# Causal mask of the plain attention scores: from TensorE's accumulation to VectorE's row-max operation

## The chip, the cores and the metric

The kernel runs on one core of a Trainium2 chip, in one launch. The metric is device time in microseconds (us). The kernel before was run three times: 2249.01, 2249.69 and 2251.82 us; its time is the median, 2249.69 us. One further execution was profiled.

## The reference, cut to what matters

Two layers of a gated cross-attention model with routed experts, on 16 sequences (batches) of 256 tokens, width 256. Only layer 0's attention changes:

```python
qh = (q @ Wq.T) ...; kh = (k @ Wk.T) ...; vh = (v @ Wv.T + bv) ...      # 16 heads of 16
scores = einsum('bhsd,bhtd->bhst', qh, kh) * scale
mask = triu(ones((Sq, Sq)), k=0).at[0, 0].set(False)
scores = where(mask, -inf, scores)
probs = softmax(scores, axis=-1)
out = einsum('bhst,bhtd->bhsd', probs, vh)
```

A token sees only the tokens before it (the first one sees itself). Layer 0's experts, layer 1's attention (with a length mask in place of the causal one) and layer 1's experts follow; the change leaves them alone.

## The kernel before, in words

The program is a row of phases: a short setup, then for each layer an attention phase, a routing phase and an expert phase. A phase begins when the one before it has ended, so a microsecond taken from layer 0's attention is one taken from the whole.

`attention_phase` (the function printed below) runs the five engines as parallel programs, tied by semaphores. Each is a software pipeline over the 16 batches (`pipeline`, with `step(i)`); in one step an engine works on several batches at once: `i.at(0)` is the batch whose output is formed, `i.at(1)` the one whose row maxima are found, `i.at(2)` the one whose queries and keys are projected, `i.at(3)` and `i.at(4)` those that are turned, normalized and loaded.

Scores are computed twice for each head. The **plain scores** (queries on partitions) serve only for the maximum of each row. The **turned scores** (keys on partitions) are computed again with the row maximum as extra rows of the stacked operands, so that ScalarE can take the exponential at once (L629) and TensorE can use the result as the operand of the product with the values (L788). In this text s(h) stands for the plain scores of head h of the next batch, t(h) for the turned scores of head h of the present batch.

Plain scores of a head fill three blocks of 128 columns of one PSUM bank: queries 0-127 by keys 0-127, queries 128-255 by keys 0-127, and queries 128-255 by keys 128-255. Before the change TensorE writes them with five matmuls of 128 columns each (L742 to L746): for the first and the third block a matmul of the identity with `mask_st` writes the mask (-1e30 above and on the diagonal), and the score matmul is added to it in PSUM. The turned scores are formed in the same way (L760 to L764). There are two banks for plain scores: s(h) waits until the maxima of head h-2 are taken (`maxed`, L738). Likewise t(h) waits for the exponential of head h-2 (L756).

The order of one step, written out by hand, is what the prediction follows:

- TensorE: query projection of `i.at(2)` (L670), turning of the max parts (L696), key projection (L670), then for h = 0 to 15: s(h), t(h); after head 4 the output projection (L711), after 6 the value projection (L679), after 8 and 9 the turnings (L660), and after heads 5, 9, 13 and 15 the products with the values of four heads (`mix_group`, L788).
- VectorE: the key copy (L470), then for each head two row maxima (L547 on 128 columns, L548 on 256), and between heads one other operation: reciprocals and divisions (L492, L498), the update of x (L507), the value copy (L517), the low parts of the turned rows (L524), the layer norm (L434, L439, L446). At the end of the step the 16 heads' maxima are cut into three bf16 parts (L558 to L565).
- ScalarE: the query copy (L605), the copy of the turned max parts (L610), and the three DMAs that lay them into `q_stack` (L614); then the 16 exponentials, with cuts and copies between them.
- t(0) waits for those three DMAs (L755).

Of the kernel before, what the change touches and what calls it, by code (L numbers as in the profile page):

```python
# [140 lines left out]
def attention_phase(nc, keep, layer, x_in, ctx_in, lens, weights, biases, scratch):  # L141
# [31 lines left out]
    with ExitStack() as ctx:  # L173
        def sb(name, shape, dt=F32):
            return ctx.enter_context(nc.sbuf_tensor(tag + name, shape, dt))
# [42 lines left out]
        if causal:  # L218
            mask_st = sb("mask_st", [P, 2, P], BF16)
            mask_ts = sb("mask_ts", [P, 2, P], BF16)  # L220
            bv_rows = sb("bv_rows", [P, TC, D])
            bo_rows = sb("bo_rows", [P, D])
        else:
            lens_i = sb("lens_i", [P, B], I32)
            lens_f = sb("lens_f", [P, B])
            iota_t = sb("iota_t", [P, S])
            neg_col = sb("neg_col", [P, 1])
            valid = sb("valid", [P, S])
            mask_row = pair("mask_row", [P, S], BF16)
# [43 lines left out]
        stacked = [sems(f"stacked_half{n}_") for n in range(2)]  # L273
        scores_done = sem("scores_done")
        maxed = sem("maxed")
        max_hi = sem("max_hi")
# [81 lines left out]
        def _(pool):  # L358
# [6 lines left out]
            if causal:  # L365
# [4 lines left out]
                nc.gpsimd.affine_select(out=mask_st[:], in_=mask_st[:], compare_op=ALU.is_gt, fill=CAUSAL_FILL,  # L370
                                        base=0, pattern=[[0, 2], [-1, P]], channel_multiplier=1).then_inc(consts_step, 1)
                nc.gpsimd.affine_select(out=mask_ts[:], in_=mask_ts[:], compare_op=ALU.is_gt, fill=CAUSAL_FILL,
                                        base=0, pattern=[[0, 2], [1, P]], channel_multiplier=-1).then_inc(consts_step, 1)
                pool.wait_ge(consts_step, 5)
                nc.gpsimd.memset(mask_st[0:1, 0, 0:1], 0.0).then_inc(consts_step, 1)
                nc.gpsimd.memset(mask_ts[0:1, 0, 0:1], 0.0).then_inc(consts_step, 1)
                pool.wait_ge(consts_step, 7)
            else:
# [37 lines left out]
        def _(dve):  # L416
# [67 lines left out]
            def step(i):  # L484
# [55 lines left out]
                for h in range(H):  # L540
                    if h == 11 and i.has(4):
                        dve.wait_ge(stats_done, i.at(4) + 1)
                    if i.has(1):
                        dve.wait_ge(scores_done, i.at(1) * H + h + 1)
                        bank = scores[h % 2]
                        if causal:
                            nc.vector.reduce_max(row_max[:, 0, h:h + 1], bank[:, 0:P], AX_X)  # L547
                            nc.vector.reduce_max(row_max[:, 1, h:h + 1], bank[:, P:3 * P], AX_X).then_inc(maxed, 1)  # L548
                        else:
                            nc.vector.reduce_max(row_max[:, :, h], bank[:].rearrange("p (c t) -> p c t", c=TC), AX_X).then_inc(maxed, 1)  # L550
                    if h in between:
                        between[h]()
# [83 lines left out]
        def _(pe):  # L636
# [97 lines left out]
            def score_head(i, h):  # L734
# [6 lines left out]
                if causal:  # L741
                    nc.tensor.matmul(bank[:, 0:P], keep.ident16[:], mask_st[:, 0, :], start=True, stop=False)  # L742
                    nc.tensor.matmul(bank[:, 0:P], q[rows, h, 0:P], k[rows, h, 0:P], start=False, stop=True)
                    nc.tensor.matmul(bank[:, P:2 * P], q[rows, h, P:S], k[rows, h, 0:P], start=True, stop=True)
                    nc.tensor.matmul(bank[:, 2 * P:3 * P], keep.ident16[:], mask_st[:, 1, :], start=True, stop=False)
                    last = nc.tensor.matmul(bank[:, 2 * P:3 * P], q[rows, h, P:S], k[rows, h, P:S], start=False, stop=True)  # L746
                else:
# [1091 lines left out]
```

## Time and profile before

| | us |
|---|---|
| median of three runs | 2249.69 |
| profiled execution, its own time | 2242.63 |
| its span from first to last instruction | 2240.9 |
| outside the span | 1.7 |

The mean granted TensorE clock over the span is 0.874 of full speed (2.4 GHz). Layer 0's attention takes about the first 560 us of the span. The profile names engines PE (TensorE matmul), PEld (its weight loads, which overlap), DVE (VectorE), ACT (ScalarE), POOL (GpSimd) and SP (SyncE). Matmuls are pipelined: the durations of their rows overlap, and the distance between starts is what one costs in a dense stretch. VectorE's rows overlap too, by a smaller amount.

### The profile page before, as it was taken

How to read it: one execution, taken by the hardware profiler on the slowest of the kernel's cores; microseconds unless marked ns; L12 is line 12 of the kernel's file. 1: busy time of each engine (PE TensorE's matmuls, PEld its weight loads, DVE VectorE, ACT ScalarE, POOL GpSimd, SP SyncE). 2: the span in 40 equal slices, each digit the busy share in tenths (PEclk: the TensorE clock that was granted, in tenths of full speed). 3: DMA queues.
4: the chain of work that ended last, by engine and by line, in shares of the span. 5: the costliest groups of instructions: out<-in, count | busy, mean ns of one | idle time of the engine just before them, and what ended most of it. 6: DMA issues, size and time to landing. Idle time of an engine off the chain costs nothing. (4 is left out here: it accounts for less than half of the span.)

```text
span 2240.9 us, 44334 instructions
## 1 busy us (share of the span) xinstructions
PE 1637.9 (73%) x14427; PEld 1343.8 (60%) x14428; DVE 1236.0 (55%) x3261; ACT 665.6 (30%) x1299; POOL 724.0 (32%) x620
## 2 busy tenths in 40 slices
PE   3787778887575477735877877787463888896897
PEld 3676667665464355533555555554342888886897
DVE  3565556554466133344656656654465566667664
ACT  2233333333464011111433333343232222221221
POOL 4121112210476455541111111110386533334332
PEclk9989998998898799976888988988676999998999
DMA  3323333321222366644323323320622233332322
GB/s 105 106 88 89 90 104 88 87 78 31 102 94 99 83 116 107 107 91 111 92 84 91 96 78 87 89 74 16 217 78 76 61 66 75 75 75 66 75 35 40
DMA packets 166676, 191.78 MB, mean 86 GB/s; under 512 B 15442, under 2 KB 146868, under 8 KB 166324
## 3 DMA queue, kind: packets, MB, share of 16 engines
q1 hardware_dynamic: 135092, 149.69, 22.9%
q0 software_dynamic: 28416, 40.03, 9.9%
q10 hardware_dynamic: 3072, 0.79, 0.2%
q8 instruction: 59, 0.97, 0.2%
q14 instruction: 37, 0.30, 0.0%
HBM read 113.73 MB, written 75.67 MB: 85 GB/s over the span
## 5 line engine op out<-in xcount | busy, mean ns | idle before, releaser
L629 ACT ACTIVATE a_probs<-a_scores_t 128x384 f32<-128x384 f32 (+1 forms) x512 | 269.7, 545 | 524.7 <-PE a_scores_t L764 262.4
L1714 ACT ACTIVATE e_hidden<-e_h,t_up_bias 128x256 f32<-128x256 f32 x348 | 145.9, 470 | 564.7 <-PE e_h L1748 552.5
L550 DVE TENSOR_REDUCE a_row_max<-a_scores 128x2 f32<-128x512 f32 x256 | 170.3, 679 | 170.5 <-PE a_scores L749 169.0
L407 POOL TENSOR_TENSOR a_rest<-a_qk,a_parts 128x1024 f32<-128x1024 f32 x32 | 68.0, 2125 | 461.6 <-ACT a_parts L582 461.6
L1639 POOL DMA_INDIRECT out_rows<-e_y,e_token x68 | 112.5, 1654 | 309.9 <-DVE e_y L1697 289.9
L1763 PE MATMUL e_y_bank<-e_down_hi,e_hidden_hi 128*128 128x256 f32 x544 | 165.1, 304 | 64.2 <-DVE e_hidden_lo L1670 63.2
L767 PE MATMUL a_scores_t<-a_q_stack,a_k_stack 101*128 101x256 bf16 x512 | 115.7, 315 | 69.0 <-DMA a_q_stack<-a_max_t 67.2
L547 DVE TENSOR_REDUCE a_row_max<-a_scores 128x1 f32<-128x128 f32 x256 | 71.5, 279 | 168.7 <-PE a_scores L746 167.4
L1763 PE MATMUL e_y_bank<-e_down_hi,e_hidden_lo 128*128 128x256 f32 x544 | 159.6, 293 | 0.0
L1763 PE MATMUL e_y_bank<-e_down_lo,e_hidden_hi 128*128 128x256 f32 x544 | 159.4, 293 | 0.0
L1748 PE MATMUL e_h<-e_xs_hi,e_up_hi 128*128 128x256 f32 x544 | 155.9, 287 | 3.1 <-DVE e_xs_lo L1660 1.9
L1670 DVE TENSOR_TENSOR e_hidden_lo<-e_hidden,e_hidden_hi 128x512 fp32r<-128x512 f32 x136 | 153.9, 1132 | 4.7
L1748 PE MATMUL e_h<-e_xs_hi,e_up_lo 128*128 128x256 f32 x544 | 155.3, 285 | 1.4 <-issue 1.4
L1748 PE MATMUL e_h<-e_xs_lo,e_up_hi 128*128 128x256 f32 x544 | 155.3, 285 | 0.4 <-issue 0.4
L1639 POOL DMA_INDIRECT x_mid_dram<-e_y,e_token x76 | 118.0, 1553 | 105.6 <-DVE e_y L1697 72.6
L1763 PEld LDWEIGHTS e_y_bank<-e_down_hi,e_hidden_hi 128*128 128x128 f32 x544 | 110.4, 203 | 69.1 <-DVE e_hidden_lo L1670 68.9
L749 PE MATMUL a_scores<-a_k_stack,a_q_stack 98*128 98x256 bf16 x512 | 115.9, 315 | 33.3 <-DMA a_k_stack<-a_mask_row 16.1
L788 PE MATMUL a_pv<-a_probs,a_v_pad 128*32 128x256 f32 (+1 forms) x2048 | 123.5, 358 | 21.4 <-ACT a_probs L629 21.4
L1151 POOL DMA_INDIRECT routed_rows_dram<-r_rows,r_slot x128 | 126.4, 987 | 38.0 <-issue 35.4
L1692 DVE TENSOR_TENSOR e_y_biased<-e_y_bank,t_down_bias 128x512 f32<-128x512 f32 x72 | 49.8, 692 | 151.4 <-PE e_y_bank L1763 135.0
L492 DVE RECIPROCAL a_den_recip<-a_pv 128x128 f32<-128x128 f32 x128 | 120.4, 944 | 18.1 <-PE a_pv L788 18.1
L1726 PE MATMUL e_turned<-ident,e_xs_rows 128*128 128x128 f32 x296 | 47.9, 285 | 105.6 <-DMA e_xs_rows<-routed_rows_dram 105.4
(257 smaller groups left out, 4539.9 us busy)
## 6 DMA issues: line engine op xcount, KB each, us to landing
parts_dram<-a_parts SPq DMA_DIRECT2D x32, 768.0 KB, 4.1
e_xs_rows<-routed_rows_dram SPq DMA_DIRECT2D x76, 258.0 KB, 2.7
a_q_stack<-parts_dram SPq DMA_DIRECT2D x64, 192.0 KB
a_k_stack<-parts_dram SPq DMA_DIRECT2D x64, 192.0 KB
a_ctx_rows<-in_ctx SPq DMA_DIRECT2D x32, 256.0 KB, 9.1
a_q_stack<-parts_dram SPq DMA_DIRECT2D x64, 128.0 KB
a_k_stack<-parts_dram SPq DMA_DIRECT2D x64, 128.0 KB
t_up<-in_L_ffn_W SPq DMA_DIRECT2D x8, 1024.0 KB, 5.2
```

What stands on the lines that cost most here:

```text
L492: nc.vector.reciprocal(den_recip[:, m, cols], pv[m][:, S + part * P:S + part * P + P]).then_inc(recip_done, 1)
L550: nc.vector.reduce_max(row_max[:, :, h], bank[:].rearrange("p (c t) -> p c t", c=TC), AX_X).then_inc(maxed, 1)
L629: nc.scalar.activation(probs[h % NP][:, 0:width], scores_t[h % 2][:, 0:width], ACT.Exp).then_inc(probs_ready, 1)
L749: last = nc.tensor.matmul(bank[:, c * S:(c + 1) * S], q[rows, h, c * P:(c + 1) * P], k[rows, h, :], start=True, stop=True)
L767: last = nc.tensor.matmul(bank[:, c * S:(c + 1) * S], k[rows, h, c * P:(c + 1) * P], q[rows, h, :], start=True, stop=True)
L788: last = nc.tensor.matmul(bank[n * VW:(n + 1) * VW, what * S + first:what * S + S], rows, probs[h % NP][:, col:col + S - first], start=(ha ...
L1151: pool.indirect_dma_start(out=xs, out_offset=bass.IndirectOffsetOnAxis(ap=slot[p][:, k, c:c + 1], axis=0), in_=rows[p][:, k, c, :], in_off ...
L1639: pool.indirect_dma_start(out=x_acc, out_offset=bass.IndirectOffsetOnAxis(ap=token[p][:, c:c + 1], axis=0), in_=y[p][:, c, :], in_offset=N ...
L1670: nc.vector.tensor_tensor(lo, src, hi.bitcast(F32), ALU.subtract).then_inc(hidden_cut, 1)
L1714: nc.scalar.activation(hidden[:, fc, :], h_bank[g][:, at:at + TS], act_func, bias=routed.up_bias[:, bass.ds(e * FC + fc, 1)]).then_inc(hid ...
L1748: last = nc.tensor.matmul(h_bank[g][:, at:at + TS], w[:, kc, fc * P:(fc + 1) * P], x[:, kc, :], start=(kc == 0 and term == 0), stop=(kc == ...
L1763: last = nc.tensor.matmul(y_bank[:, c * D:(c + 1) * D], x[:, fc, c * P:(c + 1) * P], w[:, fc, :], start=(fc == 0 and term == 0), stop=(fc ...
```

## The change

The plain scores lose their two mask matmuls, and the two blocks of queries 128-255, which share the stationary operand, become one matmul of 256 columns: two matmuls for a head in place of five. VectorE's two `reduce_max` become two `tensor_tensor_reduce`, which read the scores and the mask, write the masked scores back into the PSUM bank, and give the row maximum as accumulated output. `mask_st` becomes float32 with a third block: triangle, zeros, triangle. The wait for the scores now stands at a separate semaphore instruction (`head_taken`, which nothing waits for) in front of the pair. Turned scores, layer 1 and all else are unchanged.

```diff
-            mask_st = sb("mask_st", [P, 2, P], BF16)
+            mask_st = sb("mask_st", [P, 3, P])
...
+        head_taken = sem("head_taken")
...
                 nc.gpsimd.affine_select(out=mask_st[:], in_=mask_st[:], compare_op=ALU.is_gt, fill=CAUSAL_FILL,
-                                        base=0, pattern=[[0, 2], [-1, P]], channel_multiplier=1).then_inc(consts_step, 1)
+                                        base=0, pattern=[[0, 3], [-1, P]], channel_multiplier=1).then_inc(consts_step, 1)
...
                 nc.gpsimd.memset(mask_st[0:1, 0, 0:1], 0.0).then_inc(consts_step, 1)
+                nc.gpsimd.memset(mask_st[:, 1, :], 0.0).then_inc(consts_step, 1)
                 nc.gpsimd.memset(mask_ts[0:1, 0, 0:1], 0.0).then_inc(consts_step, 1)
-                pool.wait_ge(consts_step, 7)
+                pool.wait_ge(consts_step, 8)
...
                     if i.has(1):
-                        dve.wait_ge(scores_done, i.at(1) * H + h + 1)
                         bank = scores[h % 2]
                         if causal:
-                            nc.vector.reduce_max(row_max[:, 0, h:h + 1], bank[:, 0:P], AX_X)
-                            nc.vector.reduce_max(row_max[:, 1, h:h + 1], bank[:, P:3 * P], AX_X).then_inc(maxed, 1)
+                            dve.wait_ge(scores_done, i.at(1) * H + h + 1)
+                            dve.sem_inc(head_taken, 1)
+                            nc.vector.tensor_tensor_reduce(bank[:, 0:P], bank[:, 0:P], mask_st[:, 0, :], 1.0, CAUSAL_FILL,
+                                                           ALU.add, ALU.max, row_max[:, 0, h:h + 1])
+                            nc.vector.tensor_tensor_reduce(bank[:, P:3 * P], bank[:, P:3 * P],
+                                                           mask_st[:, 1:3, :].rearrange("p a b -> p (a b)"), 1.0, CAUSAL_FILL,
+                                                           ALU.add, ALU.max, row_max[:, 1, h:h + 1]).then_inc(maxed, 1)
...
                 if causal:
-                    nc.tensor.matmul(bank[:, 0:P], keep.ident16[:], mask_st[:, 0, :], start=True, stop=False)
-                    nc.tensor.matmul(bank[:, 0:P], q[rows, h, 0:P], k[rows, h, 0:P], start=False, stop=True)
-                    nc.tensor.matmul(bank[:, P:2 * P], q[rows, h, P:S], k[rows, h, 0:P], start=True, stop=True)
-                    nc.tensor.matmul(bank[:, 2 * P:3 * P], keep.ident16[:], mask_st[:, 1, :], start=True, stop=False)
-                    last = nc.tensor.matmul(bank[:, 2 * P:3 * P], q[rows, h, P:S], k[rows, h, P:S], start=False, stop=True)
+                    nc.tensor.matmul(bank[:, 0:P], q[rows, h, 0:P], k[rows, h, 0:P], start=True, stop=True)
+                    last = nc.tensor.matmul(bank[:, P:3 * P], q[rows, h, P:S], k[rows, h, :], start=True, stop=True)
```

## Rows read from the trace of the kernel before

**Rows 1.** The page, part 1: busy time of each engine over the span.
```profile
PE 1637.9 (73%) x14427; PEld 1343.8 (60%) x14428; DVE 1236.0 (55%) x3261; ACT 665.6 (30%) x1299; POOL 724.0 (32%) x620
```
**Rows 2.** Stretches: us, then PE, PEld, DVE, ACT, POOL busy, PEclk, DMA.
```profile
240.75:247.00 6.25, 6.25 (x53) 6.05 (x54) 3.44 (x10) 3.29 (x6) 2.13 (x1) 0.66 0.05 18
...
240.75:272.49 31.74, 25.41 (x343) 21.69 (x343) 18.53 (x53) 11.30 (x22) 6.43 (x5) 0.93 0.33 93
```
**Rows 3.** Waits from 60 to 540 us: us in total, times, longest.
```profile
DVE a_row_max L547 <- PE a_scores L746: 155.8, 108, 4.7
...
PE a_scores_t L760 <- DMA a_q_stack<-a_max_t: 59.0, 15, 4.7
```
**Rows 4.** Timeline of TensorE, one step: start us, us, what, [idle before <-releaser].
```profile
207.98 0.29 PE L760 MATMUL a_scores_t<-a_mask_ts,ident 128*128 128x128 bf16 x1 [4.69 <-DMA a_q_stack<-a_max_t]
...
211.68 0.31 PE L742 MATMUL a_scores<-a_mask_st,ident 128*128 128x128 bf16 x1
...
212.75 2.74 PE L711 MATMUL a_stage<-a_wo_t,a_heads_t 128*128 128x256 f32 x8
...
223.71 0.22 PE L742 MATMUL a_scores<-a_mask_st,ident 128*128 128x128 bf16 x1
...
224.29 0.22 PE L742 MATMUL a_scores<-a_mask_st,ident 128*128 128x128 bf16 x1
...
226.28 0.23 PE L742 MATMUL a_scores<-a_mask_st,ident 128*128 128x128 bf16 x1 [0.66 <-DVE a_row_max L548]
...
233.37 0.29 PE L696 MATMUL a_stage<-ident,a_max_parts 128*48 128x128 bf16 x2
...
240.75 0.29 PE L760 MATMUL a_scores_t<-a_mask_ts,ident 128*128 128x128 bf16 x1 [4.57 <-DMA a_q_stack<-a_max_t]
```
**Rows 5.** Timeline of VectorE in the same step, the same columns.
```profile
210.81 0.41 DVE L548 TENSOR_REDUCE a_row_max<-a_scores 128x1 f32<-128x256 f32 x1
...
224.20 0.29 DVE L547 TENSOR_REDUCE a_row_max<-a_scores 128x1 f32<-128x128 f32 x1 [1.32 <-PE a_scores L746]
224.40 0.41 DVE L548 TENSOR_REDUCE a_row_max<-a_scores 128x1 f32<-128x256 f32 x1
224.74 0.74 DVE L434 BATCH_NORM_STATS2 a_stats<-x_rows 128x6 f32 x2
225.60 0.29 DVE L547 TENSOR_REDUCE a_row_max<-a_scores 128x1 f32<-128x128 f32 x1
...
228.89 0.29 DVE L547 TENSOR_REDUCE a_row_max<-a_scores 128x1 f32<-128x128 f32 x1 [0.24 <-PE a_scores L746]
...
232.74 0.19 DVE L565 TENSOR_TENSOR a_max_parts<-a_max_rest,a_max_parts 128x32 bf16<-128x32 f32 x1
```
**Rows 6.** Timeline of ScalarE at the end of that step.
```profile
233.47 0.60 ACT L605 ACTIVATE a_qk<-a_stage 128x512 f32<-128x512 f32 x1 [3.22 <-PE a_stage L670]
233.97 0.36 ACT L610 ACTIVATE a_max_t<-a_stage 48x256 bf16<-48x256 bf16 x1
```
**Rows 7.** Layer 1's score matmul, line 749: ns min/median/max, first and last start.
```profile
L749 PE MATMUL a_scores<-a_k_stack,a_q_stack x512: 270/275/437, 1039.1 to 1541.1; 98*128 98x256 bf16 x171
```
**Rows 8.** Timeline of ScalarE in layer 1's routing: squares with an accumulated sum.
```profile
1595.46 0.38 ACT L1375 ACTIVATE r_proj_sq<-r_gated 128x256 f32<-128x256 f32 x1 [3.98 <-PE r_gated L1430]
1595.74 0.19 ACT L1375 ACTIVATION_READ_ACCUMULATOR r_proj_sq<-r_gated 128x1 f32 x1
1595.83 0.38 ACT L1375 ACTIVATE r_proj_sq<-r_gated 128x256 f32<-128x256 f32 x1
```
**Rows 9.** Groups by line and shape, 60 to 540 us: busy us, mean ns.
```profile
L517 DVE TENSOR_TENSOR a_v_pad<-a_stage,a_bv_rows 128x512 f32<-128x512 f32 x16 | 10.9, 680 | 0.0
```
**Rows 10.** The page, part 5: the expert phase's subtraction of two SBUF operands.
```profile
L1670 DVE TENSOR_TENSOR e_hidden_lo<-e_hidden,e_hidden_hi 128x512 fp32r<-128x512 f32 x136 | 153.9, 1132 | 4.7
```
**Rows 11.** Timeline of GpSimd in the setup: its last constant.
```profile
13.67 0.10 POOL L385 MEMSET a_var_eps<- 128x2 f32 x1
```
**Rows 12.** Timeline of VectorE in the setup: its last fills.
```profile
16.12 0.12 DVE L422 MEMSET a_ones_pad<- 128x16 f32 x3
```

More of the change, by code:

```diff
@@ L543, in step @@
                     if i.has(1):
-                        dve.wait_ge(scores_done, i.at(1) * H + h + 1)
                         bank = scores[h % 2]
                         if causal:
-                            nc.vector.reduce_max(row_max[:, 0, h:h + 1], bank[:, 0:P], AX_X)
-                            nc.vector.reduce_max(row_max[:, 1, h:h + 1], bank[:, P:3 * P], AX_X).then_inc(maxed, 1)
+                            dve.wait_ge(scores_done, i.at(1) * H + h + 1)
[5 more added lines that the diff above has]
+                                                           ALU.add, ALU.max, row_max[:, 1, h:h + 1]).then_inc(maxed, 1)
                         else:
+                            dve.wait_ge(scores_done, i.at(1) * H + h + 1)
                             nc.vector.reduce_max(row_max[:, :, h], bank[:].rearrange("p (c t) -> p c t", c=TC), AX_X).then_inc(maxed, 1)
```

## Prediction

> **What bounds the kernel now.** I read the page first: TensorE is busy 73% of the span, VectorE 55%, and no engine is full [rows 1]. Such an average says nothing of one phase, so I went to layer 0's attention alone. It repeats with a period, from the start of t(0) in one step to that of the next: 207.98 to 240.75, 240.75 to 272.49 [rows 2, 4]. In the second of these TensorE's rows fill 25.4 of 31.7 us, VectorE's 18.5. The waits over this phase say where the two hand over: VectorE waits 155.8 us for plain scores, in 108 of its heads, and TensorE waits 59.0 us in 15 pieces for the DMAs of the max parts [rows 3]. So a period has two parts.
>
> The **fixed part** is a chain: last row maximum, max parts (end of L565, 232.93), turning L696 (233.37), copy L610 (233.97), DMAs, t(0) at 240.75 [rows 4 to 6]. From L610 on it is 6.78 us of latency in which TensorE mostly idles. The change touches none of it.
>
> The **part of heads** runs from t(0) to L610, 26.0 us. There the timeline of TensorE shows matmuls back to back, except at one place: s(13) at 226.28 waits 0.66 us for VectorE [rows 4]. In front of it VectorE has a full row: head 10 at 224.20, the layer-norm statistics, head 11 at 225.60 [rows 5]. It is TensorE's part with VectorE close behind, and that closeness decides this change.
>
> **What TensorE saves.** From s(10) at 223.71 to s(11) at 224.29 lie ten matmuls in 0.58 us: 0.058 each [rows 4]. A 256-column matmul of layer 1 lasts 275 ns against 220 for 128 columns [rows 4, 7], that is one such step more, so the merged matmul costs what its two halves did, and a head saves the two mask matmuls: 0.115 us at 2.4 GHz, 0.213 at 1.2. s(0) lies in front of the DMA wait and saves nothing. At most 15 heads by 0.115, or 1.7 us a period, and 26 us in all over 15 periods.
>
> **What VectorE pays**, called x for a head. Before, a pair holds it 0.54 us (224.20 to 224.74), and its result is there after 0.62 (224.20 to the end of L548) [rows 5]. Streaming a second operand costs nothing: 512 columns with a PSUM and an SBUF input take 680 ns, 267 more than L548's 0.41 for 256, 1.04 ns a column, as the reductions do [rows 5, 9]. The accumulated output is the new cost. No row shows it on VectorE. On ScalarE it is an instruction of its own that puts the next start off by 0.09 us (1595.74 to 1595.83) [rows 8]. VectorE's fixed share of an instruction is 0.07 (0.20 from L547 to L548, less 128 columns at 1.04 ns), so I take 0.07 for each read and 0.01 for the pair's second operands: x = 0.15. Bounds: 0, if the read hides in the pipeline; 0.30, if each read must wait for the end of its operation (0.09 later, by L547's 0.29 against 0.20). Writing back to PSUM instead of SBUF is shown by no row; between nothing and the same 0.30 bound I take nothing.
>
> The Trainium skill, "VectorE: DVE Perf Modes", section "Two Vector instructions with no wait between them", says that an op which also writes out its accumulator is two instructions. It gives no price. Were it wrong, x would be 0.01, and the sum some 20 us down.
>
> **The separate wait.** Scores reach VectorE 0.04 us after the last matmul (it starts at 223.71 + 4 x 0.058 = 223.94, lasts 0.22, and VectorE starts at 224.20) [rows 4, 5]. Behind a wait that its sequencer holds, as head 11 behind the wait for the statistics, the start comes 0.12 after the release (225.48 to 225.60) [rows 5]. So y = 0.08 for each head whose scores VectorE awaits, and nothing where it is behind; bounds 0 and 0.15. Queued behind it stand VectorE's other operations, which are then late by as much.
>
> **The sum for one period**, in three stretches.
> *First, t(0) to the output projection (207.98 to 212.75)*, at the low clock: the granted clock of the like stretch is 0.66 [rows 2]. Masks of four heads go. The clock's rise stays about where it is, so columns count at the high clock: 4 x 0.115 = 0.46. Against it, s(4) would come at 211.68 - 3 x 0.213 = 211.04, but the maxima of head 2 end at 211.22 now [rows 4, 5], and then at 211.22 - 0.21 + y + 2x = 211.39 and a little: a wait of 0.4, worth 0.2 of high-clock work. Net -0.26.
> *Second, s(5) to s(10).* Dense on TensorE, with projections and value products that give VectorE room: 5 x 0.115 = -0.58.
> *Third, s(10) to L610.* Times from s(10) on. Scores of head 10 after 0.06 + 0.275, seen at 0.46 (before 0.49). Pair 0.69, statistics 0.92, pair result 0.76, release 0.05: s(13) at 2.88 instead of 2.57. VectorE goes on without idling: head 11 starts at 2.07, head 14 follows 3.29 - 0.24 of idling + 3x later, at 5.57 instead of 5.18 [rows 5]; the max parts end 4.04 + 2x + 0.04 after that, at 9.95 instead of 9.22. L696 and L610 follow at 0.03, 0.29 and 0.05: L610 at 10.32 instead of 10.26. The gap of 0.4 between L565's end and L696 is thus used up; the other input of L610's turn, the query projection and L605, is early by then. Net +0.08: a stretch in which three more heads' masks save nothing.
> Together -0.76. Twelve of the 15 periods have this form: -9.1. In the next two, whose steps load nothing further and leave out the layer norm, -1.4; in the last, where TensorE already waits for the maxima, -0.5. The first 16 heads, which have no turned scores beside them, are paced by the two banks; shorter scores and longer maxima cancel within 0.04 a pair: +0.3. **Sum -10.7 us.**
>
> Costed at nothing: the wider float32 mask in the setup, under 1 us more on GpSimd, which finishes at 13.8 while VectorE's fills of the same wait end at 16.2 [rows 11, 12]; without that cover it would cost its full length once. The extra `head_taken` increments have no waiter. No DMA changes.
>
> The profiled execution would go from 2242.63 to 2231.9 (span 2230.2). It stands 7.1 us under the median of the three runs, a spread I can't attribute, so against the median: 2249.69 - 10.7 = 2239.0. A difference under about 0.2% (4.5 us) can't be told from none here.
>
> **The rivals.**
> *VectorE becomes the bound (slower).* Third-stretch time grows by 6x and the first by about x: 7 us for each us of x and period, so the gain is gone at x = 0.15 + 0.76/7 = 0.26, and any more is a loss. At x = 0.30 a period is 0.29 longer, 4 us in all: 2254. For: x rests on another engine's row. 
> *TensorE stays the bound (x near 0).* Then the first stretch gives 0.46, the third 0.33 and the second 0.58: 1.4 by 15, about 20 us: 2229 (in the third, s(13) comes at 2.59, and the masks of three more heads count). Chance 0.08.
> *The clock gives it back.* TensorE has fewer columns and two new short waits in a phase whose clock falls in every period (0.66 after the wait, 0.93 over all [rows 2]). One us more at 1.2 GHz costs 0.5 us of work a period, 7.5 us in all: 2246, within 0.2%. For: periods already differ by 1 us (32.8 and 31.7) with the same work. Chance 0.20.
>
> **How the numbers follow.** Forecast 0.47; with x near 0, faster is 0.55; within 0.2% is the clock's 0.20; slower 0.25. Time 2239.0. The range takes in x near 0 with a little clock luck at its low end (2226) and x = 0.30 with the clock's 7.5 us at its high end (2262); the half-rate case is left out. The forecast's own range is 2231 to 2244.
>
> **What the profile would show.** Right: two plain score matmuls a head, of 128 and 256 columns, at the old pace; VectorE's pair at 0.65 to 0.72 us, with two short reads; a longer wait of TensorE at s(13) and a new one at s(4); L610 to t(0) still 6.3 to 6.8; VectorE's 155.8 us of waiting for scores down by a third or more; nothing changed after the phase. Wrong: a pair over 0.8 us, no read rows, periods shorter by over 1.2, a granted clock under 0.92 in the periods, or a longer DMA wait.

## The result, and the profile after

The changed kernel took 2256.26 us (median of 20 runs, 2248.97 to 2262.76), the kernel before 2249.52 us (20 runs beside them). The ratio is 1.0029, 95% interval [1.0020, 1.0039]: slower by 4.5 to 8.8 us, where -10.7 us was forecast. On another chip (experiment 9 below) it was 1.0034 [1.0020, 1.0049]. The profiled execution of the changed kernel has a span of 2253.9 us and a mean granted clock of 0.857, where before had 2240.9 and 0.874.

In the changed kernel the plain matmuls are L749 (128 columns) and L750 (256), VectorE's pair L550 and L552, the turned scores L764 to L768, the output projection L718, the turning of the max parts L703 and its copy L617. The page's first part, against [rows 1]:

```profile
PE 1625.8 (72%) x13659; PEld 1310.1 (58%) x13660; DVE 1256.0 (56%) x3773; ACT 664.4 (29%) x1299; POOL 724.5 (32%) x621
```

TensorE lost 768 matmuls and only 12 us of busy time; VectorE gained 512 instructions and 20 us. Its groups by line and shape, 60 to 540 us (busy us, mean ns of one, then idle time before them):

```profile
L552 DVE CUSTOM_DVE_ANT_0 a_scores<-a_scores,a_mask_st 128x256 f32<-128x256 f32 x247 | 115.1, 466 | 0.0
L550 DVE CUSTOM_DVE_ANT_0 a_scores<-a_scores,a_mask_st 128x128 f32<-128x128 f32 x247 | 73.6, 298 | 146.8 <-PE a_scores L750 141.5 <-DVE a_stats L436 4.0
L552 DVE DVE_READ_ACCUMULATOR2_ANT a_row_max<- 128x1 f32 x247 | 35.2, 142 | 0.0
```

and the same of the kernel before:

```profile
L548 DVE TENSOR_REDUCE a_row_max<-a_scores 128x1 f32<-128x256 f32 x253 | 104.6, 413 | 0.0
L547 DVE TENSOR_REDUCE a_row_max<-a_scores 128x1 f32<-128x128 f32 x252 | 70.3, 279 | 157.1 <-PE a_scores L746 155.8
```

Each fused operation has its read as a row of its own. What such a read costs is seen in VectorE's timeline at head 10, against the pair of [rows 5]:

```profile
225.32 0.30 DVE L550 CUSTOM_DVE_ANT_0 a_scores<-a_scores,a_mask_st 128x128 f32<-128x128 f32 x1 [0.73 <-PE a_scores L750]
225.53 0.14 DVE L550 DVE_READ_ACCUMULATOR2_ANT a_row_max<- 128x1 f32 x1
225.53 0.47 DVE L552 CUSTOM_DVE_ANT_0 a_scores<-a_scores,a_mask_st 128x256 f32<-128x256 f32 x1
225.91 0.14 DVE L552 DVE_READ_ACCUMULATOR2_ANT a_row_max<- 128x1 f32 x1
225.91 0.75 DVE L436 BATCH_NORM_STATS2 a_stats<-x_rows 128x6 f32 x2
```

The read starts in the same instant as the operation behind it, so it puts nothing off. The pair holds VectorE 0.59 us (225.32 to 225.91; 0.54 before). Its result is there after 0.73 us (to the end of the second read; 0.61 before).

**Where the time went** is in the stages of one period. Stretches of the kernel before, from t(0), s(4), s(5) and s(10), the last one up to the copy of the max parts (us; PE, PEld, DVE, ACT, POOL busy; granted clock; DMA share, GB/s). s(5) is at 215.32:

```profile
207.98:211.68 3.70, 3.70 (x35) 3.70 (x36) 2.42 (x8) 2.31 (x4) 0.38 (x1) 0.50 0.07 25
211.68:215.32 3.64, 3.64 (x20) 3.15 (x19) 1.02 (x4) 0.98 (x2) 1.75 (x1) 0.63 0.00 0
215.32:223.71 8.39, 8.39 (x135) 7.03 (x134) 4.78 (x13) 3.85 (x7) 2.14 (x1) 1.00 0.32 94
223.71:233.97 10.26, 8.71 (x140) 6.84 (x137) 8.23 (x26) 3.71 (x9) 2.16 (x3) 1.00 0.44 117
```

The same of the changed kernel (its last one runs on to the key projection, 0.25 us past the copy at 235.06):

```profile
208.96:212.42 3.46, 3.27 (x26) 2.82 (x26) 2.23 (x10) 2.34 (x5) 0.34 (x1) 0.50 0.07 25
212.42:216.77 4.35, 4.35 (x16) 3.38 (x16) 1.50 (x9) 0.84 (x2) 1.79 (x1) 0.50 0.00 0
216.77:224.80 8.03, 8.03 (x121) 6.53 (x120) 5.19 (x23) 3.85 (x7) 2.14 (x1) 0.97 0.32 91
224.80:235.31 10.51, 8.19 (x123) 6.11 (x120) 8.68 (x38) 4.04 (x9) 2.16 (x3) 1.00 0.47 120
```

and TensorE's timeline there, against [rows 4]:

```profile
208.96 0.29 PE L764 MATMUL a_scores_t<-a_mask_ts,ident 128*128 128x128 bf16 x1 [4.54 <-DMA a_q_stack<-a_max_t]
...
212.42 0.29 PE L749 MATMUL a_scores<-a_k_stack,a_q_stack 96*128 96x128 bf16 x1 [0.19 <-DVE a_row_max L552]
...
213.25 3.73 PE L718 MATMUL a_stage<-a_wo_t,a_heads_t 128*128 128x256 f32 x8
...
224.80 0.22 PE L749 MATMUL a_scores<-a_k_stack,a_q_stack 96*128 96x128 bf16 x1
...
226.12 0.23 PE L749 MATMUL a_scores<-a_k_stack,a_q_stack 96*128 96x128 bf16 x1 [0.25 <-DVE a_row_max L552]
...
227.73 0.23 PE L749 MATMUL a_scores<-a_k_stack,a_q_stack 96*128 96x128 bf16 x1 [0.99 <-DVE a_row_max L552]
...
241.74 0.29 PE L764 MATMUL a_scores_t<-a_mask_ts,ident 128*128 128x128 bf16 x1 [4.58 <-DMA a_q_stack<-a_max_t]
```

The output projection starts 4.29 us after t(0), 0.48 earlier than before (4.77): the saving is there. But it now runs wholly at 1.2 GHz (3.73 us against 2.74), and 3.52 us pass from its start to s(5) instead of 2.57. The granted clock is 0.50 in both first stretches and still 0.97 in the third; in the kernel before it had risen within the second (0.63). These rows put the loss down to the clock, and the experiments test it.

The period shown is one in which the clock rises late in both kernels. Over periods 1 to 12, the first after t(0) of batch 0 being period 0, the projection starts 4.41 us after t(0) before and 4.29 after, a saving of only 0.12, and from there to s(5) pass 1.97 and 3.11 us. The rise from 1.2 to 2.4 GHz comes 4.4 us after t(0) in the kernel before (3.1 to 6.4) and 7.2 in the changed one (6.1 to 8.6). That is more than where the fall happens to lie. Where the clock had fallen 1.6 to 2.6 us before t(0), it stayed low for 6.8 us in the kernel before (all three such periods) and in kernel 7 below (all five), and for 10.2 in the changed one (all five). TensorE also pauses in front of s(4) in all twelve periods of the changed kernel, by 0.39 to 0.40 us from one matmul's start to the next beyond their usual distance, and in none of the kernel before.

Between 75 and 550 us TensorE spent 86 us at 1.2 GHz before and 125 after. The expectations below say 85 and 132 for this; those were read from the same clock records in a window set 10 us early.

The waits from 60 to 540 us, against [rows 3]:

```profile
DVE a_scores L550 <- PE a_scores L750: 141.5, 84, 5.7
PE a_scores_t L764 <- DMA a_q_stack<-a_max_t: 55.5, 15, 4.7
...
PE a_scores L749 <- DVE a_row_max L552: 23.4, 49, 1.4
```

The last of them was 10.3 us in 18 pieces before: TensorE now waits for the maxima 49 times. The DMA wait stayed.

The 15 periods together, from copy to copy of the max parts, went from 467.4 to 473.9 us: +6.5, against +6.7 between the medians. The two profiled executions differ by more, 13.0 us of span. Of this 6.9 had come by the end of the attention phase (573.6 and 580.5), and 6.1 lie behind it, where the code is the same (1667.3 and 1673.5 us). In the four kernels of experiments 1 to 4 that same code took between 1666.0 and 1673.3 us, so I take the 6.1 as spread, not as the change's.

### The profile page after: what moved, and what is told of

It is laid out like the page before. It is cut to its first block and busy times, and to the rows that moved or that the text cites. A ratio compares the mean times of both kernels' runs of the same rounds, so it can differ in the third digit from the quotient of the medians.

```text
span 2253.9 us, 43564 instructions
## 1 busy us (share of the span) xinstructions
PE 1625.8 (72%) x13659; PEld 1310.1 (58%) x13660; DVE 1256.0 (56%) x3773; ACT 664.4 (29%) x1299; POOL 724.5 (32%) x621
## 5 line engine op out<-in xcount | busy, mean ns | idle before, releaser
L409 POOL TENSOR_TENSOR a_rest<-a_qk,a_parts 128x1024 f32<-128x1024 f32 x32 | 68.0, 2125 | 457.2 <-ACT a_parts L589 457.2
L550 DVE CUSTOM_DVE_ANT_0 a_scores<-a_scores,a_mask_st 128x128 f32<-128x128 f32 x256 | 76.4, 298 | 160.5 <-PE a_scores L750 155.2
```

## Experiments

Two theories. **Clock:** both halves of the change cost or save about what was forecast, but together they leave TensorE with too little to do after the DMA wait, and the high clock comes later. **VectorE:** its longer, later maxima simply hold TensorE up, and the clock only shows that. The twelve runs stand on three chips, on which the kernel before takes 2249.23 (runs 1 to 4), 2232.24 (5 to 8) and 2231.20 us (9 to 12). So kernels are compared by their ratios to it, or within one chip.

The table gives what each left: ratio with interval, the mean over periods 1 to 12 of the stretches in us ("wait" is copy of the max parts to t(0); "1st" t(0) to s(5); "2nd" s(5) to s(10); "3rd" s(10) to the next copy), the mean time from t(0) to the rise of the clock, the time at 1.2 GHz from 75 to 550 us, and the 15 periods together. Where the wait is filled the table gives wait and first stretch together (12.93 before, 14.02 changed); t(0) is then the first matmul behind the filling, and "rise" tells in how many of the twelve periods the clock was low during the filling. From t(0) to s(5) it was high in all of them. Each row's stretches come from one profiled execution.

| kernel | ratio to before | wait | 1st | 2nd | 3rd | rise | 1.2 GHz | 15 periods |
|---|---|---|---|---|---|---|---|---|
| before | 1 | 6.56 | 6.37 | 8.39 | 10.20 | 4.4 | 86 | 467.4 |
| changed | 1.0029 [1.0020, 1.0039] | 6.63 | 7.39 | 7.90 | 10.25 | 7.2 | 125 | 473.9 |
| 1 VectorE's half | 1.0045 [1.0028, 1.0063] | 6.60 | 6.54 | 8.39 | 10.73 | 4.8 | 90 | 478.3 |
| 2 TensorE's half | 0.9907 [0.9890, 0.9924] | 6.74 | 6.25 | 7.78 | 9.73 | 5.0 | 106 | 450.8 |
| 3 changed, filled | 0.9910 [0.9894, 0.9926] | 12.08 | with wait | 7.78 | 10.25 | none | 21 | 451.6 |
| 4 before, filled | 0.9933 [0.9917, 0.9950] | 12.08 | with wait | 8.39 | 10.20 | once | 14 | 456.4 |
| 5 TensorE's half, filled | 0.9891 [0.9865, 0.9918] | 12.52 | with wait | 7.79 | 9.73 | twice | 28 | 446.6 |
| 6 VectorE's half, filled | 1.0001 [0.9990, 1.0012] | 12.22 | with wait | 8.39 | 10.73 | none | 12 | 467.0 |
| 7 columns, heads 0-4 | 0.9995 [0.9980, 1.0010] | 6.70 | 6.30 | 7.78 | 10.65 | 4.3 | 100 | 465.8 |
| 8 held wait alone | 1.0007 [0.9996, 1.0018] | 6.67 | 6.47 | 8.39 | 10.42 | 4.7 | 85 | 473.6 |
| 9 changed again | 1.0034 [1.0020, 1.0049] | 6.64 | 7.21 | 7.87 | 10.25 | 6.8 | 123 | 471.4 |
| 10 as 7, again | 0.9991 [0.9977, 1.0005] | 6.73 | 6.28 | 7.78 | 10.38 | 4.2 | 101 | 463.7 |
| 11 columns, two places | 0.9983 [0.9968, 0.9999] | 6.72 | 6.29 | 7.78 | 10.36 | 4.0 | 91 | 462.9 |
| 12 as 3, again | 0.9929 [0.9912, 0.9946] | 12.08 | with wait | 7.78 | 10.38 | none | 23 | 451.8 |

**1. VectorE's half alone.** VectorE as in the changed kernel, TensorE with its five matmuls, the two mask operands zeros:

```diff
-                    nc.tensor.matmul(bank[:, 0:P], keep.ident16[:], mask_st[:, 0, :], start=True, stop=False)
+                    nc.tensor.matmul(bank[:, 0:P], keep.ident16[:], zero_st[:], start=True, stop=False)
...
-                    nc.tensor.matmul(bank[:, 2 * P:3 * P], keep.ident16[:], mask_st[:, 1, :], start=True, stop=False)
+                    nc.tensor.matmul(bank[:, 2 * P:3 * P], keep.ident16[:], zero_st[:], start=True, stop=False)
```

> VectorE as in the changed kernel (mask and maximum in one operation, separate wait); TensorE as before, with five matmuls a head, of which the two that wrote the mask now write zeros. Theory C (the clock): what the change lost, it lost because TensorE, with fewer columns and a pause at s(4) after the DMA wait, is granted its high clock later. With the columns back, the time at the low clock between 75 and 550 us returns from 132 us to about 85, the stretch from t(0) to s(5) from 7.35 us to about 6.5 a period, and the whole stands at 0 to 8 us over the kernel before, which is VectorE's own price. Theory V (VectorE's longer pair and its held wait set the pace): the loss of 6.7 us stays and the 10 to 15 us that the dropped masks saved are added: 16 us or more over the kernel before, and low-clock time stays above 120 us.

Measured: 2258.58 us against 2249.23, +10.1 us by the ratio, above the 0 to 8 of theory C and below the 16 of theory V. The clock's rise at 4.8 us and the first stretch (6.54) are near those of before.

**2. TensorE's half alone.** The two matmuls of the changed kernel, VectorE with its two reductions:

```diff
-                    nc.tensor.matmul(bank[:, 0:P], keep.ident16[:], mask_st[:, 0, :], start=True, stop=False)
-                    nc.tensor.matmul(bank[:, 0:P], q[rows, h, 0:P], k[rows, h, 0:P], start=False, stop=True)
...
+                    nc.tensor.matmul(bank[:, 0:P], q[rows, h, 0:P], k[rows, h, 0:P], start=True, stop=True)
+                    last = nc.tensor.matmul(bank[:, P:3 * P], q[rows, h, P:S], k[rows, h, :], start=True, stop=True)
```

> Plain scores are not masked at all (two matmuls a head, reduce_max as before, the wait on the reduction itself), so the row maxima are taken over all keys; the turned scores keep their mask. This has TensorE's saving without VectorE's price. Theory V: nothing is left that costs, the whole saving shows: 15 to 25 us under the kernel before. Theory C: stretches two and three gain (0.6 and 0.3 a period), but the clock's rise is late in part here too, since the columns are missing: low-clock time over 100 us between 75 and 550, and 3 to 13 us under the kernel before.

Measured: 2229.09 us, -20.9 us by the ratio. The time is what theory V expected (15 to 25 under) and not theory C's 3 to 13, although the low clock lasted 106 us, as C had it: TensorE's half alone loses little to the clock. The halves alone give +10.1 and -20.9, together -10.8 (by the 15 periods +10.9 and -16.6, together -5.7), and in one kernel they give +6.5. In the **third stretch** they do add: +0.53 and -0.47, and the changed kernel has +0.05. In the second, -0.61 and 0 against -0.49. In the **first** they do not: +0.17 and -0.12 against +1.02. Neither half alone moves the rise of the clock by over 0.6 us; both together move it by 2.8. Nor does either half alone show the pause in front of s(4): it is under 0.1 us in kernel 2, and 0.07 and 0.17 in two periods of kernel 1.

**3 and 4. The wait filled.** In the changed kernel and in the kernel before, 34 matmuls of 256 columns, whose result is overwritten, stand in front of the wait for the max parts (not for the first batch, where the phase has no such wait behind it):

```diff
+                if h == 0:
+                    if causal and not (isinstance(b, int) and b == 0):
+                        for _ in range(34):
+                            nc.tensor.matmul(bank[:, 0:2 * P], keep.ident16[:], mask_ts[:].rearrange("p a b -> p (a b)"), start=True, stop=True)
+                    pe.wait_ge(max_stacked[p], (i.half(0) + 1) * 48)
```

> The changed kernel with 34 matmuls of 256 columns (identity by a constant, result overwritten) put on TensorE into its wait for the DMAs of the max parts, so that it isn't idle there; work is added, none is left out. Theory C: the clock no longer falls in the periods, low-clock time between 75 and 550 us drops from 132 to under 30 us, the stretch from t(0) to s(5) from 7.35 to about 5 us, and the kernel is 25 to 35 us faster than the changed one, 18 to 28 under the kernel before. Theory V: VectorE sets the first stretch, the filling changes it by under 0.5 us a period, and the kernel stays within 7 us of the changed one.

> The kernel before with the same 34 filling matmuls in the same wait. Theory C: its low-clock time of 85 us goes too, the stretch from t(0) to s(5) falls from 6.4 to about 5.3 us: 12 to 20 us under the kernel before. Against the previous run (the changed kernel, filled) it then stands at plus 5 to 12 us, the change's gain with the clock out of the way, as forecast. Theory V: the filled kernel before is faster than the filled changed kernel.

Measured: 2228.27 and 2233.19 us, by their ratios 20 and 15 us under the kernel before. The timeline of TensorE in kernel 3:

```profile
257.22 3.88 PE L763 MATMUL a_scores_t<-a_mask_ts,ident 128*128 128x256 bf16 x34
261.85 0.23 PE L767 MATMUL a_scores_t<-a_mask_ts,ident 128*128 128x128 bf16 x1 [0.76 <-DMA a_q_stack<-a_max_t]
```

and its stretches from the copy of the max parts (255.30), the filling and the output projection:

```profile
255.30:257.22 1.92, 1.68 (x14) 1.65 (x15) 0.00 (x0) 0.36 (x2) 0.00 (x0) 1.00 0.65 204
257.22:265.38 8.16, 6.51 (x69) 5.28 (x67) 4.85 (x19) 2.58 (x5) 1.05 (x1) 1.00 0.20 62
265.38:267.16 1.78, 1.78 (x11) 1.49 (x9) 1.04 (x7) 0.49 (x1) 1.08 (x1) 1.00 0.00 0
```

The true t(0) starts at 261.85, 6.55 us after the copy, here no later than without the filling (6.78 against 6.63 over the twelve periods). The clock falls in none of the twelve periods, and 1.78 us pass from the output projection's start to s(5) instead of 3.52. Same masks, same VectorE, same DMAs: what differs is the clock, and the changed kernel's loss becomes a gain.

With the clock held the change is worth 4.9 us over kernel 4 (4.8 in the 15 periods), though the two intervals overlap. That is just under the 5 to 12 expected, and half of the 10.7 that the prediction had. The twelve periods show where: the first stretch is 5.17 us in kernel 4 and 5.30 in kernel 3, so it loses 0.13 where it was to gain.

**5 and 6. The halves with the wait filled.** The same filling in kernel 2 and kernel 1.

> Plain scores unmasked (two matmuls a head, reduce_max), and the DMA wait filled with the 34 matmuls; only the mask of the row maxima is left out. Theory C: with the clock held in all of them, savings and prices add up. The filled kernel before is 16 us under the unfilled one; TensorE's saving of 1.1 to 1.5 us a period comes in full on top: 30 to 40 us under the kernel before. Theory V: the unmasked kernel had nothing to lose on VectorE already, and filling adds what it gave the kernel before: about 36 us under. Both give nearly the same here; it is run as the version that could beat the others, and as a corner for the next run.

> VectorE's new operations, TensorE's five matmuls (zeros for the mask), DMA wait filled. Theory C: the price of VectorE's side alone with the clock held is as without filling, 7 to 11 us over the filled kernel before (which is 16 under the kernel before), so 5 to 9 us under the kernel before; and the four filled kernels (both sides old, either new, both new) fit a sum of two terms within 4 us, where the four unfilled ones miss it by 17. Theory V: they miss it by over 10 us here too, since VectorE's price would depend on how early the scores come, whatever the clock.

Measured: 2209.38 and 2232.48 us against 2232.24. Kernel 5 is the fastest of all, but leaves the mask of the maxima out. Both missed. Kernel 5 was to be 30 to 40 us under the kernel before and is 24 by its ratio; kernel 6 was to be 5 to 9 under and is level with it. Nor do the four filled kernels fit a sum of two terms within 4 us. From kernels 4, 5 and 6 the changed one, filled, should take 457.2 us for the 15 periods, and it took 451.6. By the ratios, which here stand on two chips, the miss is 11 us.

The stretches say why. Mean us over the twelve periods, with the wait apart:

| filled kernel | wait | 1st | 2nd | 3rd |
|---|---|---|---|---|
| 4 before | 6.92 | 5.17 | 8.39 | 10.20 |
| 6 VectorE's half | 6.68 | 5.54 | 8.39 | 10.73 |
| 5 TensorE's half | 7.61 | 4.91 | 7.79 | 9.73 |
| 3 changed | 6.78 | 5.30 | 7.78 | 10.25 |

With the clock held all three stretches add, the first one too: +0.37 and -0.26, and the whole has +0.13. VectorE's half costs 0.90 us a period, 0.37 in the first stretch and 0.53 in the third, and 0.91 with the masks gone (kernel 3 against kernel 5). That is 11 us over twelve periods, as in the 15 periods of kernel 6 against kernel 4 (10.6).

What does not add is the wait, and this is the filling's own cost. In kernel 5 the filling began 2.8 to 4.3 us after the copy, and in 11 of the twelve periods t(0) followed its last matmul at once, 0.11 us behind it; t(0) came 0.87 us later than in kernel 2 (7.61 against 6.74). There the filling itself delayed t(0), by most in the two periods in which the clock was low during it (9.45 and 9.70 us). In kernel 4 this happened in three periods, one at the low clock (9.52), in kernels 3 and 6 in two each. One period of kernel 5, where s(0) waits for the key transfer and the filling stands behind s(0):

```profile
257.32 0.23 PE L742 MATMUL a_scores<-a_k_stack,a_q_stack 96*128 96x128 bf16 x1 [0.95 <-DMA a_k_stack<-parts_dram]
257.50 3.88 PE L756 MATMUL a_scores_t<-a_mask_ts,ident 128*128 128x256 bf16 x34
261.21 0.22 PE L760 MATMUL a_scores_t<-a_mask_ts,ident 128*128 128x128 bf16 x1
```

**7. Columns put back after the wait only.** The changed kernel with two matmuls of 128 zero columns in heads 0 to 4 (s(0) lies in front of the wait, so eight of the ten stand behind it):

```diff
+                    fill = h <= 4 and i.has(0)
+                    if fill:
+                        nc.tensor.matmul(bank[:, 0:P], keep.ident16[:], zero_st[:], start=True, stop=False)
+                    nc.tensor.matmul(bank[:, 0:P], q[rows, h, 0:P], k[rows, h, 0:P], start=not fill, stop=True)
+                    if fill:
+                        nc.tensor.matmul(bank[:, 2 * P:3 * P], keep.ident16[:], zero_st[:], start=True, stop=True)
```

> The changed kernel with two 128-column matmuls of zeros put back into the plain scores of heads 0 to 4 of each step alone, those that follow the DMA wait. Theory C, columns decide when the clock rises: low-clock time between 75 and 550 us falls from 132 to under 105 us, the stretch from t(0) to s(5) from 7.4 to about 6.6 us, and the kernel is 5 to 12 us faster than the changed one (0 to 6 us under the kernel before), though it does more work. Rival P, the pause at s(4) decides and not the columns: low-clock time stays over 120 us, and the kernel is as slow as the changed one or up to 4 us slower.

**8. The held wait alone.** The kernel before with the separate semaphore instruction in front of its reductions:

```diff
                         if causal:
+                            dve.sem_inc(head_taken, 1)
                             nc.vector.reduce_max(row_max[:, 0, h:h + 1], bank[:, 0:P], AX_X)
```

> The kernel before with only the separate semaphore instruction in front of reduce_max (five matmuls, masks and reductions as before). It prices the wait that VectorE's sequencer holds: from the changed kernel's rows the start comes 0.20 us after the last matmul's end in place of 0.04. If the wait is the larger part of VectorE's price (9 us with the masks kept): 5 to 9 us slower than the kernel before, third stretch up by 0.3 us. If the longer operations are the larger part: under 4 us slower, third stretch up by under 0.2.

Measured: kernel 7 2232.45 us, level with before; its rise at 4.3 us and its first stretch (6.30) are back at those of before, with VectorE as slow as in the changed kernel. That rules out that VectorE's longer maxima alone make the loss. It does not separate theory C from rival P, for the added matmuls also take up the time of the pause: in front of s(4) it is gone (under 0.02 us in eleven periods, 0.11 in one).

Kernel 8 took 2234.40 us, +1.6 us by its ratio [-0.9, +4.0], with +0.22 in the third stretch of the 0.53 that VectorE's half costs there. At head 10 its reduction starts 0.15 us after the last matmul's end in all twelve periods, against 0.04 before and 0.19 in the changed kernel. By time and third stretch the held wait is the smaller part of VectorE's 10 us; but the 15 periods of its one profile are 6.2 us longer than those of before, so its share is not settled.

Kernel 7's third stretch surprised: 12.0 to 12.3 us in three of the twelve periods, 10.2 to 10.5 in the others. One of the three:

```profile
187.55:199.84 12.29, 9.78 (x122) 6.77 (x119) 8.67 (x38) 3.78 (x8) 2.16 (x3) 0.86 0.41 104
```

The granted clock is 0.86 there: it fell once more, at 190.91, when TensorE had waited 1.35 us for VectorE at s(13) (190.84). Four kernels on one chip followed.

**9. The changed kernel again.**

> The changed kernel again, on the chip of the three kernels beside it, since the eight runs so far stand on two chips whose kernel before differs by 17 us. Clock theory: ratio to before 1.001 to 1.005; the low clock between 75 and 550 us lasts about 132 us against 85, the first stretch about 7.4 us against 6.4. Rival (the loss came with one chip, and the change is a gain elsewhere): ratio 0.997 or less with the same stretches.

**10. Kernel 7 again.**

> The changed kernel with the two dropped matmuls (128 columns each, zeros) put back in heads 0 to 4 alone, again. Clock theory: some 3 to 8 us under the changed kernel beside it (first stretch 6.3 against 7.4 us, given back in part in the third, where three of twelve periods of the earlier run took 12 us instead of 10.25, each with a low clock between heads 12 and 15). Rival (the columns cost what they take and the clock gives nothing): 0 to 3 us over the changed kernel.

**11. Columns in both sparse places.** Kernel 7 with one line changed:

```diff
-                    fill = h <= 4 and i.has(0)
+                    fill = (h <= 4 or 11 <= h <= 13) and i.has(0)
```

> The same columns put back in heads 0 to 4 and in heads 11 to 13, where TensorE waits for VectorE (0.25 us at head 12, 0.99 at head 13). Clock theory: the third stretch is 10.3 to 10.5 us in every period, since the added columns lie in those waits and hold the clock; the first stretch stays at 6.3; 3 to 8 us under the kernel with the columns in heads 0 to 4 alone. Rival (the long third stretches of the earlier run have another cause, such as a late transfer): three of twelve periods still take 12 us.

**12. Kernel 3 again.**

> The changed kernel with 34 matmuls of 256 columns in the wait for the transfer before head 0's turned scores, on this chip. Clock theory: ratio to before 0.988 to 0.994, so 20 us or more under the changed kernel beside it; low clock about 24 us of the 475. Rival (what the filling bought on the first chip was that chip's): at the changed kernel's time or over it, since it adds about 3 us of TensorE work to each period.

Measured, before at 2231.20: 2238.20, 2227.96, 2230.20 and 2214.34 us. Kernel 9 repeats the loss on another chip, with the pause in front of s(4) in all twelve periods. Kernel 10 adds ten matmuls to each period and is 10.2 us faster than kernel 9, more than the 3 to 8 expected. The first two stretches of a period of kernel 9, from t(0) and from the output projection:

```profile
238.98:243.27 4.29, 4.10 (x33) 3.59 (x34) 3.06 (x15) 2.69 (x5) 1.17 (x1) 0.50 0.09 33
243.27:246.79 3.52, 3.52 (x10) 2.62 (x9) 0.67 (x5) 0.49 (x1) 0.96 (x1) 0.50 0.00 0
```

of kernel 10:

```profile
267.56:271.73 4.17, 4.17 (x42) 3.94 (x42) 3.03 (x14) 2.80 (x5) 1.15 (x1) 0.59 0.08 28
271.73:273.50 1.77, 1.77 (x11) 1.48 (x9) 0.80 (x6) 0.49 (x1) 0.98 (x1) 1.00 0.00 0
```

More work, and done sooner: the output projection at 2.4 GHz takes 1.77 us instead of 3.52. Kernel 11 had no long third stretch (10.3 to 10.8 in all twelve), but kernel 10 had only one this time, of 12.07 us:

```profile
312.00:324.07 12.07, 9.75 (x122) 6.95 (x119) 8.68 (x38) 3.78 (x8) 2.16 (x3) 0.86 0.40 112
```

So the step of 3 to 8 us that was expected between them did not come (2230.20 against 2227.96, intervals overlapping), and one against none doesn't show what those columns do. Kernel 12, which has no added columns in its heads, had one as well (12.05 us, the clock low from 309.5 to 312.9), so they don't come from the columns of heads 0 to 4. Kernel 12 is 23.9 us under kernel 9 and, by its ratio, 15.8 under before: of the kernels that compute the whole, the changed one with the filled wait is the fastest.

Giving the fused operation its wait directly, without the separate instruction, wasn't tried. Nor was a kernel with few columns behind the wait, slow maxima and no pause in front of s(4), or one with the columns kept and the pause put in: whether columns or the pause delay the rise stays open.

## Why the prediction was wrong, step by step

**The step that failed** is in the first stretch: "The clock's rise stays about where it is, so columns count at the high clock". It was put at -0.26 us up to the output projection. That part came out at -0.12 over the twelve periods (-0.48 in the period shown), but the rise moved from 4.4 to 7.2 us after t(0), and up to s(5) the stretch is 1.02 us longer, 12 us over twelve periods. My own rows said that the clock falls in every period [rows 2]; I took its rise as given, though kernels 7 and 10 show that it follows from what TensorE does after the wait, which is just what the change thins out.

**A second error lies in the same term.** With the clock held the first stretch does not gain either: 5.17 us before, 5.30 after (kernels 4 and 3). TensorE's saving there is 0.26 and VectorE's price 0.37. The forecast let VectorE cost one wait at s(4), worth 0.2. So even without the clock's loss the change is worth about 5 us and not 10.7.

**Second stretch.** Forecast -0.58, measured -0.49, and -0.61 in kernel 2, where the clock has risen by then. Right; the missing 0.1 is the clock again.

**Third stretch.** Forecast +0.08 (10.32 instead of 10.26), measured +0.05. In the period shown s(13) comes 2.93 us after s(10) (forecast 2.88, before 2.57), and the copy at 235.06, 10.26 after s(10). Right: three heads' masks save nothing there, VectorE takes them. Kernels 1 and 2 show both sides of that balance, +0.53 and -0.47.

**x** was 0.15 us. Occupancy rose by 0.05 to 0.06 and the result's delay by 0.12. The estimate from ScalarE's accumulator read let each read put the next start off; on VectorE it starts with the next operation. The Trainium skill, "VectorE: DVE Perf Modes", section "Two Vector instructions with no wait between them", has the operation with an accumulator as two instructions; the trace agrees, with 142 ns for the second. The rule on halved rate (the Trainium skill, "Vector Engine (DVE) Microarchitecture Reference", "Points that are easy to get wrong") spares this form, and the trace agrees: 466 ns for 256 columns against 413 for the reduction.

**y** was 0.08 us. At head 10 the last matmul ends at 225.13 (224.86 from the timeline, plus 0.27), and VectorE starts at 225.32: 0.19 against 0.04, so y = 0.15, the upper bound. The errors in x and y offset each other. The sum of the two halves measured alone is -10.8 us by their ratios, next to the forecast sum of -10.7. That is in part luck: by the 15 periods it is -5.7, and each ratio's interval is 4 us to either side. The terms of the second and third stretch were good, that of the first was not.

**The other terms.** The last three periods +0.5 us (forecast -1.9), the first one -1.7; the first copy of the max parts came 1.0 us later (forecast +0.3), but 0.5 earlier in kernel 9, so I don't put it down to the change. The fixed part stayed: 6.56 and 6.63.

**The rivals.** "The clock gives it back" was the right one, at 0.20, and too small: it priced one us more at 1.2 GHz a period. It was 2.8; 39 us more in all (125 less 86), which at half speed is up to 19.5 us of work, against the 17 us by which halves and whole differ (12 by the 15 periods). It had also named the new wait at s(4). "VectorE becomes the bound" had the right sign with the wrong cause: the pair is shorter than I took it, and kernel 10, with that same VectorE, is not slower than before. Its extreme, the half rate, did not occur.

**The signs named in advance.** Seen: two matmuls a head, short reads, waits at s(4) (0.19) and s(13) (0.99), the same fixed part. "Nothing changed after the phase" can't be read from two executions, which differ by 6.1 us there. Not seen: a pair of 0.65 to 0.72 (0.59), and VectorE's 155.8 us of waiting down by a third (141.5, since longer periods gave some of it back). The sign for wrong was there: a granted clock of 0.86 over 208.96 to 241.74, under the 0.92.

The Trainium skill, "TensorE: Matmul & The Clock Gate", Part 1, says that the low clock is the default state and activity lifts it. Kernels 12 and 10 agree: each does more than the changed kernel, never falls at the wait or rises earlier, and is 24 and 10 us faster than kernel 9. Exactly what TensorE must do after the wait for an early rise stays open: with few columns alone (kernel 2, 5.0 us) or slow maxima alone (kernel 1, 4.8) it was early, with both (7.2) it was not. Both together are also the only case with a pause of 0.4 us in front of s(4), so the pause explains these kernels as well as the columns do.

## What to carry to other kernels

In a phase whose clock falls at a wait in every period, cost an edit twice: once for its instructions, and once for when the clock rises, since columns that leave the stretch behind the wait, or a pause that opens in it, may cost more than the edit saves. Test the parts of a change alone and together; where the stretches of one profile add up and one does not, that stretch holds the cause. Compare them by stretch, since whole times carry several us of spread from code that the change never touched. And before trimming such a stretch, fill the wait in front of it with matmuls that nobody needs: it was worth 15 us to the kernel before and 24 to the changed one. Check then that the filling ends before the wait does. In kernel 5 it mostly did not, and t(0) came 0.87 us later in a period than unfilled, against 0.15 in kernel 3.

## What the hardware did that was not expected

- VectorE's accumulator read (142 ns) starts in the same instant as the next operation; it delays only the result.
- With a wait held by an instruction of its own, VectorE's reduction started 0.15 us after the last matmul (kernel 8) and its fused operation 0.19 (changed, kernels 1 and 9), against 0.04 where the reduction itself waited.
- The granted clock could fall within the heads too: at s(13) in three of twelve periods of kernel 7 and in one each of kernels 10 and 12, which made that stretch 1.5 to 2 us longer.
- With the clock held, both halves' effects added in every stretch within 0.02 us; without, the first stretch missed the sum by 1 us.
- The kernel before took 2249.23, 2232.24 and 2231.20 us on three chips, 0.8% apart, more than anything the change does. For the changed kernel, 13.5 us of the 17.4 between its two profiled executions (changed and 9) lie behind the attention phase. Its ratio was nearly the same on both, 1.0029 and 1.0034.
